# The causal mask of the second score pass: GpSimd selects on the probabilities in place of mask products on TensorE

## The chip, the cores and the metric

The kernel runs on one core of a Trainium2 chip. The metric is device time in microseconds, of one execution of the whole program. Engines are named as in the profile: PE is TensorE's products, PEld its weight loads, DVE is VectorE, ACT is ScalarE, POOL is GpSimd, SP is the queue that issues most DMAs.

## What is computed

Two blocks in a row on an input of 2 batches of 512 tokens with 128 channels. The first (an HGRN block with quantised linear layers and a conditioning path) is untouched by the change. The second is a transformer block with adaptive layer norms; its attention has 16 heads of width 8 and a causal mask:

```python
def _attention(x, Wqkv, Wproj, bproj):
    ...
    scores = jnp.einsum('bhqd,bhkd->bhqk', q, k) * scale
    causal = jnp.tril(jnp.ones((t, t), bool))
    scores = jnp.where(causal, scores, -jnp.inf)
    attn = jax.nn.softmax(scores, axis=-1)
    out = jnp.einsum('bhqk,bhkd->bhqd', attn, v)
    ...
...
x = x + gt_a[:, None, :] * _attention(xm, Wqkv, Wproj, bproj)
xn = _layernorm(x, g2, be2)
...
h = jax.nn.gelu(xm @ W1 + b1, approximate=False)
x = x + gt_m[:, None, :] * (h @ W2 + b2)
```

## The kernel before

The program is written engine by engine, with semaphores set by hand; each engine goes through its instructions in the order of the text. The attention works in 8 groups of 4 heads (2 batches, 4 groups each; `N_GROUPS`). The heads of a group stand in two halves of the partitions, rows 0 to 63 and 64 to 127, so that products of the two halves can run beside each other in PE's array. Queries and keys are split into three bf16 parts and stacked (`QS`, `KS`, 48 rows of a half).

Scores are computed twice. The **first pass** has queries on the partitions: for each group there are 12 score items (`score_item`, lines 1401 to 1403), each one score product for one or two heads and then two mask products, which add -1e30 above the diagonal. An item goes to one of three PSUM banks, and DVE takes its row maxima (`row_maxima`, line 1139). When the 12 items of a group are reduced, DVE splits the maxima into three bf16 parts by four small operations (`split_maxima`, lines 1149 to 1152), PE transposes them (`maxima`, line 1413), DVE copies them (line 1160), and SP's DMAs put them into `QS` as three more rows (line 358).

The **second pass** has keys on the partitions. Its score product (51 rows, the maxima included) gives the score less its row's maximum. It goes in 5 slots for a group (`exp_slot`): slots 0 and 1 hold key tile 0, slots 2 and 3 key tiles 1 and 3, slot 4 key tile 2. A slot fills two banks; banks 0 to 3 are used in turn by slot. Before the change each pair of tiles has a score product for either half (line 1437) and then two mask products for either half (lines 1440 and 1443), which write into the first 128 columns of the tile, the diagonal block:

```python
for half in range(2):
    rows = half_rows(2 * half, XROWS)
    T.matmul(dsts[half], KS[b][rows, h, tok(kt)], QS[b][rows, h, kt * P:L], start=True, stop=False)
for half in range(2):
    r = half_rows(2 * half)
    T.matmul(dsts[half][:, 0:P // 2], k_of("pickLo", r), k_of("maskKlo", r), start=False, stop=False)
```

ACT takes the exponential of a slot into `PT` (line 707) and counts `p_ready`. PE waits for `p_ready` of two slots before when it fills a slot again, and for the slots of a key tile before that tile's value products (`values`, line 1457; `PV_SLOTS` has the count). The value matrix carries a column of ones, so the sum of each row comes out of the same products. ACT copies the result (line 715), PE turns it (line 1290, helper `to_columns`), and DVE divides (lines 1168, 1169).

The order of the rounds is written by hand. In round n PE does the 12 score items of group n; between them stand slots 3 and 4 of group n-2 (at items 1 and 4), slots 0, 1 and 2 of group n-1 (at items 7, 9, 11), the transposes of the maxima of group n-1 (at item 2), the value products of group n-2 (key tiles 0, 1, 3, 2 at items 5, 6, 7, 10), and the turned values of group n-3 (at item 3). The loop runs on for three rounds after the last group; in round 8 PE also does the attention columns and the projection of batch 0, and at the end of round 9 the transposes of its normalised rows (`norm_columns(0)`).

POOL has little to do in this stage. It issues half of the DMAs that stack the keys, adds the projection's bias to `xs`, and later, for each batch, takes the root for the norm (line 379) when DVE has the variance (`ln_var`), waits until DVE has written the normalised rows (`xhat_ready`), and adds the bias of the MLP to `xs` (line 470).

## Time and profile before

| what | value |
|---|---|
| median of 3 runs | 289.58 us (289.57 to 290.57) |
| profiled execution, its own time | 289.72 us |
| its span in the profile | 287.60 us |
| granted TensorE clock, mean | 0.798 |
| PE / PEld busy | 160.0 us (56%) / 102.1 us (35%) |
| DVE busy | 188.6 us (66%) |
| ACT busy | 139.1 us (48%) |
| POOL busy | 69.5 us (24%) |
| chain that ended last | DVE 37%, PE 33%, DMA 10%, POOL 5%, SP 5%, ACT 4% |

Busy times are shares of the whole span. The program has stages with different limits, so these shares do not say what a change in one stage is worth. PE's products are pipelined and their ends are modelled; starts are the better guide there.

### The profile page before, as it was taken

What the parts mean: (1) busy time and instruction counts of PE and PEld (TensorE: products, weight loads), DVE (VectorE), ACT (ScalarE), POOL (GpSimd) and SP (SyncE); (2) the same over time, 40 slices, a digit from 0 to 9 for tenths busy, and PEclk for the clock granted to TensorE, in tenths of its full rate; (3) what the DMA queues carried; (4) which work ended last, traced back from release to release, by engine and by line L of the source; (5) the groups of instructions that cost most, each with busy time, mean ns of one, the idle gap of its engine ahead of it and who ended that gap; (6) DMA issues with size and microseconds to landing.
All of it is one profiled execution on the core that took longest, in us unless ns stands there. A gap on an engine that the chain in (4) does not pass through costs nothing.

```text
span 287.6 us, 4182 instructions
## 1 busy us (share of the span) xinstructions
PE 160.0 (56%) x1493; PEld 102.1 (35%) x1495; DVE 188.6 (66%) x528; ACT 139.1 (48%) x297; POOL 69.5 (24%) x77
## 2 busy tenths in 40 slices
PE   0212239444733006227580009579999999897985
PEld 0102135243512003027350006254564456354664
DVE  0687797999966985965852009657897788715320
ACT  3455877557845036933164000045466446676621
POOL 7061621326035152960168000000000000003110
PEclk9999999857555556857777555559999999999999
DMA  6992000000000000000048555500000000000010
GB/s 190 417 396 125 1 0 0 0 2 1 0 0 1 0 0 0 1 2 0 0 72 89 69 69 72 70 4 4 4 3 1 5 4 2 4 2 3 0 39 36
DMA packets 5355, 12.15 MB, mean 42 GB/s; under 512 B 1075, under 2 KB 3604, under 8 KB 4692
## 3 DMA queue, kind: packets, MB, share of 16 engines
q1 hardware_dynamic: 4758, 11.09, 14.8%
q0 software_dynamic: 576, 0.79, 2.1%
q8 instruction: 12, 0.20, 0.3%
q14 instruction: 9, 0.07, 0.1%
HBM read 8.11 MB, written 0.52 MB: 30 GB/s over the span
## 4 chain that ended last, share of the span: by engine, by line
DVE 37%; PE 33%; DMA 10%; POOL 5%; SPq 5%; ACT 4%; issue 4%; DVEq 0%; ACTq 0%
DVE negmax L1139 9%; PE ps L1457 6%; DMA KS<-part 6%; PE ps L1290 5%; SPq L326 4%; PE ps L1401 4%; POOL uh L445 3%; DMA QS<-nmT 3%; PE ps L1487 2%; PE ps L1493 2%; DMA cw<-in_cond_w 2%; PE ps L1349 2%; PE ps L1437 2%; DVE xhat L810 2%; DVE u L967 2%
## 5 line engine op out<-in xcount | busy, mean ns | idle before, releaser
L1139 DVE TENSOR_REDUCE negmax<-ps 128x1 f32<-128x384 f32 (+3 forms) x96 | 52.6, 594 | 35.7 <-PE ps L1403 35.7
L707 ACT ACTIVATE PT<-ps 128x1024 f32<-128x1024 f32 x40 | 40.7, 1026 | 63.8 <-PE ps L1443 63.6
L1401 PE MATMUL ps<-KS,QS 48*128 48x384 bf16 (+3 forms) x128 | 36.5, 344 | 21.1 <-DMA KS<-part 20.8
L379 POOL TENSOR_TENSOR rstd<-veps,mhalf 128x4 f32<-128x4 f32 x8 | 8.1, 1016 | 139.9 <-DVE veps L804 139.9
L1290 PE MATMUL ps<-k_f,u 128*128 128x128 f32 x40 | 10.0, 426 | 34.4 <-ACT u L631 23.4
L1437 PE MATMUL ps<-QS,KS 51*128 51x512 bf16 (+3 forms) x128 | 24.6, 315 | 5.1 <-DMA QS<-nmT 5.0
L1402 PE MATMUL ps<-k_b 64*128 64x128 bf16 x128 | 27.2, 245 | 0.0
L1401 PEld LDWEIGHTS ps<-KS,QS 48*128 48x128 bf16 x128 | 11.7, 100 | 37.5 <-issue 22.5
L1403 PE MATMUL ps<-k_b 64*128 64x64 bf16 x128 | 23.9, 208 | 0.0
L1457 PE MATMUL ps<-PT,V 128*9 128x512 f32 (+3 forms) x256 | 22.5, 434 | 1.9 <-ACT PT L707 1.2
L1290 PEld LDWEIGHTS ps<-k_f,u 128*128 128x128 f32 x40 | 7.6, 221 | 36.2 <-DVE u L967 28.1
L1443 PE MATMUL ps<-k_b 64*128 64x128 bf16 x128 | 18.2, 222 | 0.0
L1440 PE MATMUL ps<-k_b 64*128 64x64 bf16 x128 | 17.5, 196 | 0.0
L1403 PEld LDWEIGHTS ps<-k_b 64*128 64x128 bf16 x128 | 13.2, 111 | 6.7 <-issue 2.4
L379 POOL TENSOR_TENSOR rms<-vms,mhalf 128x4 f32<-128x4 f32 x10 | 10.2, 1033 | 21.0 <-DVE vms L941 20.8
L1220 PE MATMUL ps<-k_f,cq 2*128 2x2 f32 x14 | 2.3, 249 | 19.0 <-DVE cq L830 19.0
L810 DVE TENSOR_SCALAR xhat<-xs,bnmv,rstd 128x128 f32<-128x128 f32 x32 | 10.8, 401 | 3.0 <-POOL rstd L379 2.9
L1402 PEld LDWEIGHTS ps<-k_b 64*128 64x128 bf16 x128 | 12.2, 104 | 0.0
L1437 PEld LDWEIGHTS ps<-QS,KS 51*128 51x128 bf16 x128 | 9.4, 96 | 7.1 <-DMA QS<-nmT 6.0
L1349 PE MATMUL ps<-k_f,uh 128*128 128x128 f32 x32 | 6.4, 386 | 9.7 <-DVE uh L1102 9.7
L445 POOL TENSOR_TENSOR uh<-prod,brow 128x512 f32<-128x512 f32 x8 | 9.8, 1270 | 5.2 <-DVE prod L1089 5.2
L1443 PEld LDWEIGHTS ps<-k_b 64*128 64x128 bf16 x128 | 9.2, 98 | 3.0 <-issue 0.6
(200 smaller groups left out, 435.0 us busy)
## 6 DMA issues: line engine op xcount, KB each, us to landing
w<-in_wa SPq DMA_DIRECT2D x2, 1152.0 KB, 10.7
QS<-part SPq DMA_DIRECT2D x24, 64.0 KB
brow<-in_bcast_rows SPq DMA_DIRECT2D x1, 1152.0 KB, 15.9
lw<-in_l_w SPq DMA_DIRECT2D x1, 1152.0 KB
mw<-in_main_w SPq DMA_DIRECT2D x1, 1024.0 KB, 13.5
KS<-part POOLq DMA_DIRECT2D x12, 64.0 KB, 5.6
KS<-part SPq DMA_DIRECT2D x12, 64.0 KB
cw<-in_cond_w SPq DMA_DIRECT2D x1, 576.0 KB, 5.9
```

The lines of the kernel that those rows point to most:

```text
L379: return nc.gpsimd.tensor_tensor(r, v, mhalf[0:v.shape[0], 0:v.shape[-1]], ALU.pow)
L445: nc.gpsimd.tensor_tensor(uh[b][:, t, :], prod[b][t % 2][:, :], brow_of("nm2"), ALU.mult).then_inc(S["uh_raw"], 1)
L707: nc.scalar.activation(PT[n % 2][:, s, :], bank(2 * (use % 2), 2), ACT.Exp).then_inc(S["p_ready"], 1)
L1139: V.tensor_reduce(negmax[n % 2][:, qt, h0:h0 + nh], bank(S_BANKS[k % 3])[:, 0:nh * w].rearrange("p (h w) -> p h w", w=w), AX.X, ALU.max, n ...
L1290: ins = T.transpose(dst[:, tok(t)], src(t), ident)
L1401: T.matmul(dst, QS[b][rows, h, tok(qt)], KS[b][rows, h, 0:w], start=True, stop=False)
L1402: T.matmul(dst[:, w - P:w], k_of("pickLo", r), k_of("maskQlo", r), start=False, stop=False)
L1403: ins = T.matmul(dst[:, w - P // 2:w], k_of("pickHi", r), k_of("maskQhi", r), start=False, stop=True)
L1437: T.matmul(dsts[half], KS[b][rows, h, tok(kt)], QS[b][rows, h, kt * P:L], start=True, stop=False)
L1440: T.matmul(dsts[half][:, 0:P // 2], k_of("pickLo", r), k_of("maskKlo", r), start=False, stop=False)
L1443: ins = T.matmul(dsts[half][:, 0:P], k_of("pickHi", r), k_of("maskKhi", r), start=False, stop=True)
L1457: ins = T.matmul(bank(6)[32 * j:32 * j + HD + 1, kt * P:L], V1[b][:, kt, g * HG + j, :], src, start=(kt == 0), stop=(kt == 2))
```

## The change

The mask products of the second pass are taken out. ACT's exponential now counts `p_exp`, on which PE's reuse of the banks waits. POOL waits for the same count, sets the upper triangle of each diagonal block of `PT` to zero by `affine_select`, in place, and counts `p_ready`, on which the value products wait as before. The two mask tables of this pass leave the constants. The first pass keeps its mask products. POOL's root and addition for batch 0's norm (`norm_root(0)`) now stand behind the select of slot 2 of the last group, those of batch 1 at the end.

```diff
 KC, KC_N = _spans(("ident", P), ("pickLo", P), ("pickHi", P), ("maskQlo", P), ("maskQhi", P // 2),
-                  ("maskKlo", P // 2), ("maskKhi", P), ("count", 16))
+                  ("count", 16))
...
-            for b in range(B):
+
+            def drop_future(n, s):
+
+                diagonals = [(0, 2, L)] if s < 2 else [(0, 2, L), (3 * P, 2, L)] if s < 4 else [(0, 4, 2 * P)]
+                pool.wait_ge(S["p_exp"], 5 * n + s + 1)
+                for at, count, step in diagonals:
+                    v = PT[n % 2][:, s, :].rearrange("p (c w) -> p c w", w=step)[:, :, at:at + P]
+                    ins = nc.gpsimd.affine_select(v, v, [[0, count], [1, P]], ALU.is_ge, 0.0, base=0,
+                                                  channel_multiplier=-1)
+                ins.then_inc(S["p_ready"], 1)
+
+            def norm_root(b):
                 pool.wait_ge(S["ln_var"], 3 * B + b + 1)
                 root(rstd[:, tiles(b)], veps[:, tiles(b)]).then_inc(S["ln_root"], 1)
 
                 pool.wait_ge(S["xhat_ready"], B + b + 1)
                 nc.gpsimd.tensor_tensor(xs[:, tiles(b), :], xs[:, tiles(b), :], over_tiles(b2_g[:, b, :]), ALU.add
                                         ).then_inc(S["biased"], 1)
+
+            for n in range(N_GROUPS):
+                for s in range(5):
+                    drop_future(n, s)
+                    if n == N_GROUPS - 1 and s == 2:
+                        norm_root(0)
+            norm_root(1)
...
                 nc.scalar.activation(PT[n % 2][:, s, :], bank(2 * (use % 2), 2), ACT.Exp
-                                     ).then_inc(S["p_ready"], 1)
+                                     ).then_inc(S["p_exp"], 1)
...
                 if use >= 2:
-                    pe.wait_ge(S["p_ready"], use - 1)
+                    pe.wait_ge(S["p_exp"], use - 1)
...
-                        T.matmul(dsts[half], KS[b][rows, h, tok(kt)], QS[b][rows, h, kt * P:L], start=True, stop=False)
-                    for half in range(2):
-                        r = half_rows(2 * half)
-                        T.matmul(dsts[half][:, 0:P // 2], k_of("pickLo", r), k_of("maskKlo", r), start=False, stop=False)
-                    for half in range(2):
-                        r = half_rows(2 * half)
-                        ins = T.matmul(dsts[half][:, 0:P], k_of("pickHi", r), k_of("maskKhi", r), start=False, stop=True)
+                        ins = T.matmul(dsts[half], KS[b][rows, h, tok(kt)], QS[b][rows, h, kt * P:L],
+                                       start=True, stop=True)
                 ins.then_inc(S["st_pe"], 1)
```

How the change moves instructions is seen in the order in which they stand on an engine. First POOL, at the end of the program, before the change: L379 is the root, L470 the addition, for batch 0 and then batch 1.

```order
L463 TENSOR_TENSOR xs<-xs,bproj_g 128x512 [waits xhat_ready,gated]
L463 TENSOR_TENSOR xs<-xs,bproj_g 128x512
L379 TENSOR_TENSOR rstd<-veps,mhalf 128x4 [waits ln_var]
L470 TENSOR_TENSOR xs<-xs,b_g 128x512 [waits xhat_ready]
L379 TENSOR_TENSOR rstd<-veps,mhalf 128x4 [waits ln_var]
L470 TENSOR_TENSOR xs<-xs,b_g 128x512 [waits xhat_ready]
```

The same end after the change (L472 is the select, L481 the addition), from the first three slots of the last group on:

```order
L472 AFFINE_SELECT PT<-PT 128x2x128 [waits p_exp] x3
L472 AFFINE_SELECT PT<-PT 128x2x128
L379 TENSOR_TENSOR rstd<-veps,mhalf 128x4 [waits ln_var]
L481 TENSOR_TENSOR xs<-xs,b_g 128x512 [waits xhat_ready]
L472 AFFINE_SELECT PT<-PT 128x2x128 [waits p_exp]
L472 AFFINE_SELECT PT<-PT 128x2x128
L472 AFFINE_SELECT PT<-PT 128x4x128 [waits p_exp]
L379 TENSOR_TENSOR rstd<-veps,mhalf 128x4 [waits ln_var]
L481 TENSOR_TENSOR xs<-xs,b_g 128x512 [waits xhat_ready]
```

The selects of slots 3 and 4 of the last group stand behind an addition that waits for DVE's normalised rows. Second PE, in a round, around slot 0 of a group and the value products of key tile 3, before:

```order
L1437 MATMUL ps<-QS,KS 128x512 [waits p_ready,nm_stacked0]
L1437 MATMUL ps<-QS,KS 128x512
L1440 MATMUL ps<-k_b 128x64 x2
L1443 MATMUL ps<-k_b 128x128 x2
L1457 MATMUL ps<-PT,V 9x128 [waits p_ready]
L1457 MATMUL ps<-PT,V 9x128 x3
```

And after (L1455 is the score product, L1470 the value product):

```order
L1455 MATMUL ps<-QS,KS 128x512 [waits p_exp,nm_stacked1]
L1455 MATMUL ps<-QS,KS 128x512
L1470 MATMUL ps<-PT,V 9x128 [waits p_ready]
L1470 MATMUL ps<-PT,V 9x128 x3
L1419 MATMUL ps<-KS,QS 128x512 [waits s_used]
```

Four products between the scores and what follows are gone, and nothing else changed its place on PE.

## Rows read from the trace of the kernel before

**Rows 1.** The page: busy time, and granted clock and GB/s in 40 slices.

```profile
PE 160.0 (56%) x1493; PEld 102.1 (35%) x1495; DVE 188.6 (66%) x528; ACT 139.1 (48%) x297; POOL 69.5 (24%) x77
...
PEclk9999999857555556857777555559999999999999
...
GB/s 190 417 396 125 1 0 0 0 2 1 0 0 1 0 0 0 1 2 0 0 72 89 69 69 72 70 4 4 4 3 1 5 4 2 4 2 3 0 39 36
```

**Rows 2.** By stretch: us; PE, PEld, DVE, ACT, POOL busy; clock, DMA share, GB/s.

```profile
221.58:231.32 9.74, 9.04 (x143) 5.06 (x138) 7.86 (x20) 5.48 (x7) 0.00 (x0) 1.00 0.01 4
```

**Rows 3.** Chain of waits through one round: start, us, what.

```profile
222.78 0.39 PE ps L1413 x4
...
224.76 0.10 PE ps L1443 x2
...
226.60 0.76 PE ps L1457 x8
...
227.78 0.19 PE ps L1440
...
228.80 2.49 DVE negmax L1139 x4
```

**Rows 4.** The same chain before the projection of batch 0.

```profile
257.89 0.03 PE ps L1440 x2
257.92 0.06 PE ps L1443 x2
```

**Rows 5.** PE in order of time, slot 2 of a group: start, us, instruction.

```profile
229.87 0.33 PE L1437 MATMUL ps<-QS,KS 51*128 51x384 bf16 x1
```

**Rows 6.** POOL's instructions by form: busy us, mean ns, idle before.

```profile
L445 POOL TENSOR_TENSOR uh<-prod,brow 128x512 f32<-128x512 f32 x8 | 9.8, 1270 | 5.2 <-DVE prod L1089 5.2
L379 POOL TENSOR_TENSOR rstd<-veps,mhalf 128x4 f32<-128x4 f32 x8 | 8.1, 1016 | 139.9 <-DVE veps L804 139.9
...
L384 POOL TENSOR_SCALAR w4q<-w,whalf 128x768 bf16<-128x768 f32 x2 | 4.4, 2198 | 0.0
L374 POOL MEMSET KS<- 128x2048 f32 x2 | 3.5, 1798 | 0.0
...
L384 POOL TENSOR_SCALAR cwq<-cw,whalf 128x640 bf16<-128x640 f32 x1 | 1.9, 1890 | 2.0 <-DVE whalf L769 2.0
...
L423 POOL TENSOR_TENSOR wproj_g<-lw,gates 128x128 f32<-128x128 f32 x2 | 0.9, 462 | 0.0
```

**Rows 7.** ACT and DVE in order of time, end of one round.

```profile
230.77 1.02 ACT L707 ACTIVATE PT<-ps 128x1024 f32<-128x1024 f32 x1 [0.62 <-PE ps L1443]
...
231.32 0.17 DVE L1149 CAST nmpart<-negmax 128x16 bf16<-128x16 f32 x1
...
231.95 0.17 DVE L1152 TENSOR_TENSOR nmpart<-nmrest,nmpart 128x16 bf16<-128x16 f32 x1
```

**Rows 8.** DVE and POOL in order of time, an earlier stage.

```profile
59.77 0.17 DVE L950 SCALAR_TENSOR_TENSOR stepq<-amax,guard 128x12 f32<-128x12 f32 x1
...
65.51 1.28 POOL L427 TENSOR_TENSOR w_g<-lw,gates 128x512 f32<-128x512 f32 x1
65.61 1.21 DVE L950 SCALAR_TENSOR_TENSOR stepq<-amax,guard 128x12 f32<-128x12 f32 x1
```

**Rows 9.** POOL and PE in order of time, after the last group.

```profile
261.54 1.03 POOL L379 TENSOR_TENSOR rstd<-veps,mhalf 128x4 f32<-128x4 f32 x1 [103.97 <-DVE veps L804]
...
262.09 2.34 PE L1457 MATMUL ps<-PT,V 128*9 128x512 f32 x32 [1.20 <-ACT PT L707]
...
263.80 1.27 POOL L470 TENSOR_TENSOR xs<-xs,b_g 128x512 f32<-128x512 f32 x1 [1.23 <-DVE xhat L810]
```

**Rows 10.** PE in order of time, after an idle stretch of an earlier stage.

```profile
69.80 1.54 PE L1290 MATMUL ps<-k_f,u 128*128 128x128 f32 x6 [3.00 <-DVE u L967]
```

**Rows 11.** PE by form, 127 to 133 us, and 264 to 273 us.

```profile
L1349 PE MATMUL ps<-k_f,uh 128*128 128x128 f32 x24 | 5.4, 423 | 9.7 <-DVE uh L1102 9.7
...
L1290 PE MATMUL ps<-k_f,xhat 128*128 128x128 f32 x4 | 0.7, 286 | 0.0
```

More of the change, by code:

```diff
@@ L128 @@
     "minv_ready", "mod_copied", "mod_pe", "mod_ready", "mx_ready", "niT_pe", "ni_ready", "nm_ready", "o_ready",
-    "p_ready", "par_ready", "part0", "part1", "part2", "pr_pe", "prod_ready", "pv_pe", "pv_ready", "qk_pe",
+    "p_exp", "p_ready", "par_ready", "part0", "part1", "part2", "pr_pe", "prod_ready", "pv_pe", "pv_ready", "qk_pe",
     "rest_ready", "s_pe", "s_used", "sg_ready", "sig_ready", "silu_c", "st_pe", "stack_init", "stored", "ug_ready",
@@ L1570 @@
     mask_q = _np.where(i[None] > i[:, None], f32(BIG), f32(0))
-    mask_k = _np.where(i[:, None] > i[None], f32(BIG), f32(0))
     counts = _np.array([1.0 / WCOUNT[name] for name in WCOL] + [0.0] * (16 - len(WCOL)), f32)
@@ L1585 @@
         "rows1": _np.concatenate([a["L1_bada"][2 * D:3 * D], a["L1_bada"][5 * D:]])[None],
-        "consts": _np.concatenate([eye, eye[lo], eye[hi], mask_q[lo], mask_q[hi][:, P // 2:], mask_k[lo][:, :P // 2],
-                                   mask_k[hi], _np.broadcast_to(counts, (P, 16))], 1),
+        "consts": _np.concatenate([eye, eye[lo], eye[hi], mask_q[lo], mask_q[hi][:, P // 2:],
+                                   _np.broadcast_to(counts, (P, 16))], 1),
     }
```

## The prediction

> **What bounds the kernel now.** I read the page first. No engine is full over the span [rows 1], so an average tells little and the stage has to be looked at. The change works in the attention stage, from about 189 us on. Its rounds are alike: one of the five full ones stands in the table by stretch [rows 2]; each is 9.74 us with DVE busy 7.86 us and PE busy about 9 (pipelined, so not at its peak), and POOL not at all. The chain of waits through one round then says who ends last [rows 3]: it goes through DVE from the first 512-wide reduction of a round (228.80) over the four small splitting operations to the first reduction behind them, and through PE from the transposes of the maxima (222.78) to 228.80. So what PE does between 222.78 and 228.80 is on the path, and what it does beside the four long reductions and the splitting operations is not.
>
> **Mask products off PE.** A group has 8 pairs of score blocks (one block in each half), each with 2 mask products a half: 32 products leave each group, 256 in all, with their weight loads. The two halves stand in different rows of the array and run beside each other, so a pair costs what one half costs. Two clean pieces of the chain show it: 0.03 + 0.06 = 0.09 us from the end of the score product to the next work [rows 4]. In the PE stretch of a round lie slot 4 (two pairs, chain piece 224.76) and slot 0 (one pair, 227.78); slots 1, 2 and 3 lie beside DVE's reductions, slot 2 at 229.87 for instance [rows 3, 5]. That is 3 x 0.09 = 0.27, I take 0.28 us for each of six rounds (groups 2 to 7): **-1.7 us**. The first round runs at half the clock and is partly DVE-bound; I give it **-0.2**. The last round waits for a DMA of the maxima, which hides what was saved before it; the four pairs between it and the projection (0.37 us) I count in the tail below.
>
> **Smaller constants.** 192 columns of 784 go, 98 KB. The second weight load lands behind them and ACT waits for it; the page's slices moved 190 to 417 GB/s [rows 1], so 98 KB are 0.24 to 0.5 us: **-0.2**. The cast of the constants is shorter too, on an idle DVE, worth nothing. No DMA is passed: POOL's stacking DMAs stand ahead of the selects.
>
> **What a select costs.** The trace has none. The nearest rows are POOL's [rows 6]: two-input operations of 512 elements 1.27 us and of 128 elements 0.47, so 2.1 ns an element and 0.73 us for 256; a one-input comparison of 768 in 2.20, of 640 in 1.89, so 2.4 ns an element, 0.97 us for 256 and 1.58 for 512; a fill of 2048 in 1.80, which leads to about 0.3 and 0.5. I take 0.85 us for 256 and 1.43 for 512, between the two that read; the fill, which reads nothing, and the comparison are the ends. What speaks for something far dearer is the power function, 1.02 us for four elements. The Trainium skill (GPSIMD Engine Reference, Engine selection) calls one-input work "roughly line-rate"; at the 1.2 GHz it gives, that would be an estimated 0.2 us and the issue for 256, near the fill and against the comparison's row. By that page the sum below would end near 291.
>
> **Does POOL keep up?** Seven selects in a group, six of 256 and one of 512: 6 x 0.85 + 1.43 = 6.5 us of a 9.7 us round. The tight place is slot 3. Slot 2's exponential ends at 231.79 in the round shown [rows 7]; the value products that want slot 3 start at 226.60 in this round [rows 3], so at 236.34 in the next; between them POOL has four selects, 4.5 us, so a select may cost 1.1 us before PE waits. PE's own bank reuse waits for the exponential alone and is untouched. So in a round these waits are hidden; cover gone, they cost 4c - 4.5 us a round.
>
> **The new collision.** Slot 2's exponential ends at 231.79, and without the masks of slots 1 and 2 (3 x 0.09 us of PE work before it) near 231.5. POOL then starts two selects. DVE's four splitting operations run from 231.32 to 232.12 [rows 7], and two of them read two tiles of SBUF. The trace of another stage shows what happens then [rows 8]: the small operation of line 950 takes 0.17 us when POOL is idle and 1.21 us when it starts 0.10 us behind a POOL operation of 1.28 us: it is held until that one ends. Line 1152 would start at 231.95 and be held to 231.55 + 0.85 = 232.40: 0.45 us, on the chain, in six rounds: **+2.7**. Nothing if the select falls behind it; if line 1150 is caught as well, up to one more select, 1.3 us a round. The Trainium skill (SBUF — State Buffer, Who interferes with whom) goes further: copies and casts that enter a two-port mode are held as well. The casts of lines 1149 and 1151 have no row beside a busy POOL; by that page the collision would be nearer the dear end, some 2 to 5 us more in the sum.
>
> **The tail.** This is the largest term. The changed order on POOL puts the root and the addition of batch 0's norm ahead of the selects of the last group's slots 3 and 4. The root waits for DVE's statistics and starts at 261.54, the addition waits for the normalised rows, starts at 263.80 and takes 1.27 us, ending at 265.07 [rows 9]. With the 0.37 us from the mask products before the projection (257.89 and its like, [rows 4]) it ends at 264.70. Only then come two selects of slot 3, to 266.40. The value products of key tile 1 (0.76 us) start, key tile 3 follows (0.34); slot 4's select ends at 267.83; key tile 2 (0.55, from the like rows of a round) is done at about 268.45. Before, the 32 value products ended at 262.09 + 2.34 = 264.43 [rows 9]. Everything behind them (PE's in-order queue: the transposes of batch 0's normalised rows, those of the values, the projection of batch 1, the MLP) waits for PE: **+4.0 us**, from 2.6 with selects priced as the fill to 4.4 with those priced as the comparison.
>
> **The clock.** In that tail PE stands idle for some 3.8 us, and before that for 1.2 as now [rows 9]. Earlier in the run an idle of 3.00 us that ended at 69.80 [rows 10] took the granted clock down: PEclk in the page is 7 in the slice around it and 5, the lower of the two levels (1.2 instead of 2.4 GHz), in the five slices behind it [rows 1]. A 128x128 f32 product takes 423 ns at the low level and 286 at the high one [rows 11], some 1.5 times. With four to five us of such work at the low level, of which part is hidden: **+1.5**, from 0 to 3.
>
> **Sum.** -1.7 - 0.2 - 0.2 + 2.7 + 4.0 + 1.5 = +6.1 us. The profiled execution took 289.72 us (span 287.60 and 2.12 around it), 0.14 above the median of 289.58, which I leave out. 289.7 + 6.1 = **295.8 us**.
>
> **Rivals.** *The collision misses.* The selects start behind line 1152 or do not hold it; the end of slot 2's exponential is only 0.16 us from that line's start now. Then -2.1 + 4.0 + 1.0 gives 292.6; with selects priced as the fill, 2.6 of tail and 0.5 of clock, 290.7. *POOL becomes the bound.* With a select of 1.5 us (2.6 for the wide one) POOL needs 11.6 us a round, two more than now: 6 x 2 for rounds, 5 to 6 in the tail and 3 for clock and collision give about 310. It decides from 1.1 us a select; POOL's idle column and the comparison row speak against it, the power function for it. *Faster.* The mask products give back more than the chain says: PE's work beside the reductions counts too, so that all 8 pairs of a group shorten a round, 8 x 0.09 = 0.72 us, in seven rounds 5.0. With selects priced as the fill, tail 2.6 and clock 0.5, no collision, the time is 289.7 - 0.4 - 5.0 + 3.1 = 287.4. It decides where the gain of a round passes 0.4 us. Against it: beside the reductions PE waits for DVE's banks, not DVE for PE, since DVE's idle time of a round lies before 228.80 and not behind it.
>
> **Chances and range.** A measurement of this kernel tells about 0.5% (1.45 us) from no change. Forecast 0.58, collision missed 0.21 (0.06 of it within 0.5%), POOL the bound 0.13, faster 0.08 (0.06 beyond 0.5%, 0.02 within). That is faster 0.06, same 0.08, slower 0.86. The forecast's own ends: low with a light collision 292; high with 4.4 of tail, 3 of clock and a collision of 1.1 us in six rounds, 6.6: -2.1 + 14.0, 301.6. The range reaches to 290.8 for the missed collision and to 303 for a POOL that just binds; what lies outside is the faster case and most of the POOL-bound one, about 0.2.
>
> **What would show it.** Right: rounds of about 9.9 us instead of 9.74, with DVE's line 1152 at 0.5 to 0.7 us instead of 0.17 and the transposes of the maxima later by that; selects at 0.7 to 1.0 us; in the tail, selects directly behind the b2 addition, PE idle for over 3 us between the first and the second set of value products and waiting for POOL, and a granted clock below 1.00 behind it. Wrong: a round shorter than 9.5 us with line 1152 at 0.17 (collision missed); rounds over 10.5 us with POOL near full and PE waiting for selects inside them; or no PE wait for POOL in the tail, which would take the largest term away.

## The result and the profile after

| | before | after |
|---|---|---|
| median of 4 runs each | 289.57 us (289.02 to 290.57) | 299.27 us (298.16 to 303.03) |
| ratio | | 1.032 (1.027 to 1.037) |
| profiled execution, its span | 289.72 us, 287.6 us | 298.16 us, 296.0 us |
| granted TensorE clock, mean | 0.798 | 0.758 |

The changed kernel is slower by 3.2%. Measured once more in a later session it took 300.54 us against 288.82 (ratio 1.035, 1.027 to 1.043). The forecast was 295.8 us in a range of 290.8 to 303.0: the sign and roughly the size came out, but two large terms were missing that nearly cancel. Ratios leave out runs over 1.5% above the fastest of their kernel, which flatters a kernel whose own runs spread further than that, so medians of all runs stand beside them.

The spans show the two missing terms. They are cut at three events that both traces have: the first score product of the second pass, DVE's first splitting operation of group 1, and DVE's first splitting operation of the last group. The last stretch, from that operation to the end, is called the tail below, and times "in the tail" count from it.

| stretch | before | after | difference | forecast |
|---|---|---|---|---|
| start of the program to the first score product of the second pass | 188.90 | 179.81 | -9.1 | -0.2 |
| to the first splitting operation of group 1 | 3.91 | 3.75 | -0.2 | -0.2 |
| six rounds, to the first splitting operation of group 7 | 57.99 | 70.02 | +12.0 | +1.0 |
| tail | 36.8 | 42.4 | +5.6 | +5.5 |
| sum | 287.6 | 296.0 | +8.4 | +6.1 |

The page of the changed kernel, the lines that answer to [rows 1]; the fourth line is the group of all selects:

```profile
PE 171.3 (58%) x1237; PEld 97.4 (33%) x1239; DVE 191.2 (65%) x528; ACT 138.3 (47%) x297; POOL 93.3 (32%) x133
...
PEclk9999999756655558667975555598777796895999
...
GB/s 184 409 403 88 1 0 0 0 3 0 0 1 0 0 0 1 0 2 0 50 101 87 88 98 7 4 1 3 2 3 2 4 0 4 2 3 0 0 38 35
...
L472 POOL TENSOR_SCALAR_AFFINE_SELECT PT<-PT 128x256 f32<-128x256 f32 (+1 forms) x56 | 23.8, 439 | 83.8 <-ACT PT L725 83.8
```

PE has 256 products fewer and is busy 11.3 us longer. That contradiction is the first thing to see: the products that stay must have become slower. The clock's digits say why. In [rows 1] they are 9 from 195 us on to the end; now the slices of the rounds have 6 to 9, most of them 7 or 8.

**The rounds.** By stretch, two rounds of the changed kernel (the columns of [rows 2]: us; PE, PEld, DVE, ACT, POOL busy; granted clock, DMA share, GB/s):

```profile
206.42:217.49 11.07, 10.07 (x106) 4.71 (x104) 8.36 (x19) 5.38 (x7) 2.98 (x7) 0.85 0.01 3
217.49:230.01 12.52, 11.52 (x106) 5.08 (x104) 8.46 (x19) 5.39 (x7) 2.98 (x7) 0.73 0.01 2
```

Against [rows 2], a round has its 32 mask products fewer (a window's count takes in a few at its edges) and lasts 1.3 to 2.8 us longer, and its mean clock is 0.85 or 0.73 where it was 1.00. POOL is busy 2.98 us of 11 to 12.5, so it bounds nothing. Cut finer, the same view shows a mean of 0.85 to be one stretch of 3.4 us at the lower level, 1.2 GHz (in the rounds at 0.73 it is 6.8 us):

```profile
207.00:208.00 1.00, 0.14 (x4) 0.14 (x4) 0.96 (x4) 1.00 (x2) 0.45 (x2) 1.00 0.00 0
208.00:209.00 1.00, 1.00 (x12) 0.76 (x11) 1.00 (x4) 0.02 (x1) 0.77 (x2) 0.88 0.00 0
209.00:210.00 1.00, 1.00 (x6) 0.51 (x5) 0.84 (x3) 0.00 (x0) 0.00 (x0) 0.50 0.00 0
210.00:211.00 1.00, 1.00 (x14) 0.61 (x15) 0.96 (x4) 0.15 (x1) 0.00 (x0) 0.50 0.02 6
211.00:212.00 1.00, 1.00 (x8) 0.00 (x0) 0.49 (x1) 0.87 (x1) 0.06 (x1) 0.50 0.02 6
212.00:213.00 1.00, 1.00 (x11) 0.33 (x11) 0.10 (x1) 0.00 (x0) 0.57 (x1) 0.91 0.00 0
213.00:214.00 1.00, 1.00 (x13) 0.26 (x5) 0.46 (x1) 0.00 (x0) 0.00 (x0) 1.00 0.00 0
```

The fall comes behind PE's one wait of the round. In order of time on PE that wait is this row, 0.86 us before the transposes of the maxima:

```profile
207.87 0.39 PE L1431 MATMUL ps<-k_b,nmpart 128*12 128x128 bf16 x4 [0.86 <-DVE negmax L1157]
```

Before, the same wait was 0.61 us (213.04 us and the same place of the other rounds), and the clock stayed at 1.00. From round to round the fall comes 0.1 to 1.8 us behind the end of this wait. So the trace alone leaves two suspects: a longer wait, or fewer products around it.

**The collision.** DVE in order of time at the end of one round, then POOL at the same time:

```profile
217.49 0.17 DVE L1167 CAST nmpart<-negmax 128x16 bf16<-128x16 f32 x1
217.70 0.18 DVE L1168 TENSOR_TENSOR nmrest<-negmax,nmpart 128x16 f32<-128x16 f32 x1
217.91 0.28 DVE L1169 CAST nmpart<-nmrest 128x16 bf16<-128x16 f32 x1
218.23 0.32 DVE L1170 TENSOR_TENSOR nmpart<-nmrest,nmpart 128x16 bf16<-128x16 f32 x1
...
217.76 0.76 POOL L472 TENSOR_SCALAR_AFFINE_SELECT PT<-PT 128x256 f32<-128x256 f32 x2 [1.06 <-ACT PT L725]
```

It happens, at the instruction that was named: L1170 (the old L1152) takes 0.32 us where [rows 7] have 0.17. The cast of L1169 is held too, 0.28 instead of 0.17. Together that is 0.11 + 0.15 = 0.26 us more a round, where 0.45 was forecast.

**The tail.** PE in order of time behind the last group (the rows that answer to [rows 9]), then POOL:

```profile
266.25 1.43 PE L1470 MATMUL ps<-PT,V 128*9 128x512 f32 x8 [1.12 <-DVE attn L1187]
270.01 2.75 PE L1470 MATMUL ps<-PT,V 128*9 128x384 f32 x24 [2.33 <-POOL PT L472]
...
265.71 1.04 POOL L379 TENSOR_TENSOR rstd<-veps,mhalf 128x4 f32<-128x4 f32 x1 [1.26 <-DVE veps L822]
267.98 1.26 POOL L481 TENSOR_TENSOR xs<-xs,b_g 128x512 f32<-128x512 f32 x1 [1.23 <-DVE xhat L828]
269.19 1.36 POOL L472 TENSOR_SCALAR_AFFINE_SELECT PT<-PT 128x256 f32<-128x256 f32 x3
```

The selects stand directly behind the b2 addition (the addition of the MLP's bias), and PE waits 2.33 us for them, with 24 of the 32 value products behind the wait. Stretches of 2 us show PE idle throughout 268 to 270. The clock is at its lower level there, but it fell before this wait began, at 266.78 us, which is why the first stretch has 0.70:

```profile
266.00:268.00 2.00, 1.43 (x8) 0.15 (x8) 1.22 (x5) 0.20 (x1) 0.77 (x2) 0.70 0.00 0
268.00:270.00 2.00, 0.00 (x0) 0.00 (x0) 0.00 (x0) 0.00 (x0) 2.00 (x4) 0.50 0.00 0
270.00:272.00 2.00, 1.99 (x20) 0.76 (x24) 0.00 (x0) 0.00 (x0) 0.55 (x1) 0.50 0.00 0
```

**The start.** The chain of waits runs through the stacking DMAs in both kernels; first the last piece of one wait in the changed kernel:

```profile
154.64 12.72 DMA KS<-part
```

and the same piece before:

```profile
156.13 15.96 DMA KS<-part
```

A second piece of this kind, DMA QS<-nmT, takes 6.27 us before and 1.91 after and ends at 188.86 and at 179.76. So of the 9.1 us 1.5 lie ahead of the first piece, 3.2 in it and 4.4 in the second. The GB/s of the full slices there are 69 to 89 before [rows 1] and 87 to 101 after. The stacking, which the change doesn't touch, landed sooner.

### The profile page after: what moved, and what is told of

Its sections match the earlier page's. It is cut to its first block, busy times and chain, and to the rows that moved or that the text cites. A ratio compares the mean times of both kernels' runs of the same rounds, so it can differ in the third digit from the quotient of the medians.

```text
span 296.0 us, 3727 instructions
## 1 busy us (share of the span) xinstructions
PE 171.3 (58%) x1237; PEld 97.4 (33%) x1239; DVE 191.2 (65%) x528; ACT 138.3 (47%) x297; POOL 93.3 (32%) x133
## 4 chain that ended last, share of the span: by engine, by line
DVE 40%; PE 35%; DMA 8%; POOL 7%; issue 4%; ACT 4%; SPq 2%; DVEq 0%
DVE negmax L1157 9%; PE ps L1470 9%; PE ps L1308 5%; DMA KS<-part 4%; PE ps L1419 4%; POOL uh L445 3%; DMA w<-in_wa 3%; PE ps L1500 2%; PE ps L1506 2%; DVE xhat L828 2%; PE ps L1455 2%; DVE bnst L815 2%; DVE u L985 2%; DVE mx L1068 2%; PE ps L1367 1%
## 5 line engine op out<-in xcount | busy, mean ns | idle before, releaser
L472 POOL TENSOR_SCALAR_AFFINE_SELECT PT<-PT 128x256 f32<-128x256 f32 (+1 forms) x56 | 23.8, 439 | 83.8 <-ACT PT L725 83.8
L1419 PE MATMUL ps<-KS,QS 48*128 48x128 bf16 (+3 forms) x128 | 40.4, 371 | 16.4 <-DMA KS<-part 15.4
L1470 PE MATMUL ps<-PT,V 128*9 128x512 f32 (+3 forms) x256 | 32.6, 600 | 4.0 <-POOL PT L472 2.3
L1420 PE MATMUL ps<-k_b 64*128 64x128 bf16 x128 | 29.6, 261 | 0.0
L1421 PE MATMUL ps<-k_b 64*128 64x64 bf16 x128 | 25.6, 220 | 0.0
L1455 PE MATMUL ps<-QS,KS 51*128 51x512 bf16 (+3 forms) x128 | 25.0, 340 | 0.6 <-DMA QS<-nmT 0.6
L379 POOL TENSOR_TENSOR rstd<-veps,mhalf 128x4 f32<-128x4 f32 x8 | 8.3, 1036 | 40.6 <-DVE veps L822 40.6
L1421 PEld LDWEIGHTS ps<-k_b 64*128 64x128 bf16 x128 | 14.5, 120 | 9.3 <-issue 5.3
L379 POOL TENSOR_TENSOR rms<-vms,mhalf 128x4 f32<-128x4 f32 x10 | 10.2, 1031 | 21.0 <-DVE vms L959 20.8
L1420 PEld LDWEIGHTS ps<-k_b 64*128 64x128 bf16 x128 | 12.7, 107 | 1.4 <-issue 0.6
L1367 PE MATMUL ps<-k_f,uh 128*128 128x128 f32 x32 | 5.6, 350 | 9.7 <-DVE uh L1120 9.7
L604 ACT ACTIVATE junk<-mx 128x128 f32<-128x128 f32 x16 | 4.7, 297 | 11.1 <-DVE mx L954 11.1
L379 POOL TENSOR_TENSOR cs<-cs,mhalf 2x1 f32<-2x1 f32 x6 | 3.4, 558 | 20.7 <-DVE cs L838 20.7
L1455 PEld LDWEIGHTS ps<-QS,KS 51*128 51x128 bf16 x128 | 8.5, 101 | 3.2 <-issue 2.2
## 6 DMA issues: line engine op xcount, KB each, us to landing
w<-in_wa SPq DMA_DIRECT2D x2, 1152.0 KB, 10.5
```

The lines of the kernel that those rows point to most:

```text
L379: return nc.gpsimd.tensor_tensor(r, v, mhalf[0:v.shape[0], 0:v.shape[-1]], ALU.pow)
L472: ins = nc.gpsimd.affine_select(v, v, [[0, count], [1, P]], ALU.is_ge, 0.0, base=0, channel_multiplier=-1)
L1419: T.matmul(dst, QS[b][rows, h, tok(qt)], KS[b][rows, h, 0:w], start=True, stop=False)
L1420: T.matmul(dst[:, w - P:w], k_of("pickLo", r), k_of("maskQlo", r), start=False, stop=False)
L1421: ins = T.matmul(dst[:, w - P // 2:w], k_of("pickHi", r), k_of("maskQhi", r), start=False, stop=True)
L1455: ins = T.matmul(dsts[half], KS[b][rows, h, tok(kt)], QS[b][rows, h, kt * P:L], start=True, stop=True)
```

## The experiments

Each ratio is against the kernel before in the same session (medians 288.40 to 288.82 us), with its 95% interval. The medians are of all runs; for the close cases both are read.

**e1: selects kept, mask products put back.** The changed kernel's order, waits and POOL work, with the four mask products of a pair and their two tables as before.

```diff
-                        ins = T.matmul(dsts[half], KS[b][rows, h, tok(kt)], QS[b][rows, h, kt * P:L],
-                                       start=True, stop=True)
+                        T.matmul(dsts[half], KS[b][rows, h, tok(kt)], QS[b][rows, h, kt * P:L], start=True, stop=False)
+                    for half in range(2):
+                        r = half_rows(2 * half)
+                        T.matmul(dsts[half][:, 0:P // 2], k_of("pickLo", r), k_of("maskKlo", r), start=False, stop=False)
+                    for half in range(2):
+                        r = half_rows(2 * half)
+                        ins = T.matmul(dsts[half][:, 0:P], k_of("pickHi", r), k_of("maskKhi", r), start=False, stop=True)
```

> The changed kernel with the mask products of the second pass and their tables put back: PE works as before the change, POOL selects as after it. Theory (the clock): the slower rounds of the changed kernel come from the granted clock, which falls when PE has less to do; with the products back it stays at 1.00 in the rounds, a round takes 9.74 us plus what the selects cost DVE's splitting operations (0 to 0.3 us), and the sum is 289.6 + 6 x 0.2 + the tail behind the root and addition (about 3) = 294. Rival (the selects): the selects themselves stretch the rounds, by holding DVE or PE; then a round stays at 11 to 12.5 us and the time stays at 299 or goes above it.

Measured: 292.77 us (290.91 to 293.66), ratio 1.013 (1.007 to 1.019). Two of its rounds, by stretch, and PE's wait in the first of them:

```profile
207.79:217.70 9.91, 9.05 (x143) 5.06 (x138) 8.03 (x19) 5.48 (x7) 2.97 (x7) 1.00 0.01 3
217.70:227.60 9.90, 9.04 (x143) 5.05 (x138) 8.03 (x19) 5.47 (x7) 2.98 (x7) 1.00 0.02 4
...
209.15 0.39 PE L1431 MATMUL ps<-k_b,nmpart 128*12 128x128 bf16 x4 [0.77 <-DVE negmax L1157]
```

256 more products, and the kernel is 6.5 us faster than the changed one's 299.27. Its start was 3.2 us later than the changed kernel's (182.98 against 179.81 us), so the gain doesn't come from there: its six rounds take 60.5 us against 70.0. All its rounds from the second of the six on are 9.90 us at clock 1.00. PE waits 0.77 us in them, longer than the 0.61 of before, and the clock holds. POOL works as long as in the changed kernel, so POOL is not what lengthens the rounds there. What is left over 9.74 is 0.17 us, the collision: in its rounds only the last splitting operation is held (0.34 us instead of 0.17), since with the masks back the selects start later against the splitting. The tail stays long (43.3 us), as it should with the order on POOL unchanged; PE waits 2.71 us for the selects in it, and the clock is at its lower level for 10.2 us from the midst of that wait.

**e2: no masks and no selects.** The kernel before with the mask products taken out and nothing in their place; the exponential's scale is set to 0.1 so that future tokens do not overflow. The second pass is then not causal.

```diff
-                        T.matmul(dsts[half], KS[b][rows, h, tok(kt)], QS[b][rows, h, kt * P:L], start=True, stop=False)
...
+                        ins = T.matmul(dsts[half], KS[b][rows, h, tok(kt)], QS[b][rows, h, kt * P:L], start=True, stop=True)
```

> The kernel before without the mask products of the second pass and without selects, so that the second pass has no causal mask; the exponential's scale is 0.1 so that its values stay finite. POOL does nothing in the rounds. Theory (the clock): the granted clock falls in the rounds as in the changed kernel, rounds of 10.5 to 12 us, about 297 in all. Rival (the selects): rounds shorten to about 9.45 us as the chain of the kernel before says, and the time is 289.6 - 2 = 287.5.

Measured: 294.30 us (289.72 to 297.41, 10 runs), ratio 1.013 (1.008 to 1.018). Work was taken away, none was added, and it is slower than before. Two of its rounds, by stretch:

```profile
223.97:233.63 9.66, 8.62 (x106) 4.27 (x104) 7.87 (x20) 5.39 (x7) 0.00 (x0) 1.00 0.01 2
233.63:244.40 10.77, 10.02 (x106) 4.73 (x104) 8.10 (x20) 5.39 (x7) 0.00 (x0) 0.84 0.01 3
```

The clock falls without any POOL work, and with PE's wait for the maxima at 0.61 us as before. So the fewer products are enough, and the wait of 0.86 us isn't needed for it; nor is a longer wait alone enough, by the 0.77 us of e1. Over its ten executions the mean granted clock was 0.762 to 0.794, over the 13 of the kernel before 0.793 to 0.815, so this is no matter of the one trace. Its rounds swing between 9.66 at 1.00 and 10.77 at 0.84; those of the changed kernel go down to 0.73, which the longer wait behind the collision may explain; fewer products with nothing but a longer wait weren't run. The row at full clock carries a second result: taking the masks away is worth 9.74 - 9.66 = 0.08 us a round, not 0.28. PE in order of time says where the rest went, first the value products of key tile 0 in the round of [rows 2], then the same in this one:

```profile
225.21 1.04 PE L1457 MATMUL ps<-PT,V 128*9 128x512 f32 x8
...
227.59 1.05 PE L1451 MATMUL ps<-PT,V 128*9 128x512 f32 x8 [0.30 <-DVE attn L1169]
```

PE now comes to the value products before DVE has divided the previous group's turned values, which lie in the same bank, and waits 0.30 us for it. No full round of the kernel before has this wait. Against the first splitting operation of the round the value products start at 3.63 us before (225.21 - 221.58) and at 3.62 here (227.59 - 223.97): taking away the two pairs of masks of slot 4, which stand ahead of them, gained nothing. The one pair of slot 0 stands behind them and gave the 0.08: the next 512-wide reduction of DVE starts at 7.22 us before (228.80) and 7.14 here (231.11).

**e4: filler products.** The changed kernel with six 512-column products a round, whose results nobody reads, ahead of the transposes of the maxima, so that PE's wait there is filled (0.21 us of it are left).

```diff
+            def filler(n):
+                use = 5 * n + 4
+                pe.wait_ge(S["p_exp"], use - 1)
+                for half in (0, 1) * 3:
+                    r = half_rows(2 * half, SROWS)
+                    T.matmul(bank(2 * (use % 2) + half), KS[0][r, 0, tok(0)], QS[0][r, 0, :], start=True, stop=True)
...
+                    if i == 2 and 2 <= n < N_GROUPS:
+                        filler(n - 2)
```

> The changed kernel with six 512-column products a round that nobody reads (rounds 2 to 7), written into the banks of slot 4 ahead of its scores, where PE waits for DVE anyway (before the transposes of the maxima): per half 1536 columns, as many as the mask products had. Theory (the clock): the granted clock stays at 1.00 in the rounds, rounds of 9.7 to 9.9 us instead of 11.0 to 12.5, 299.3 - 6 x 1.7 = 289 and with the tail unchanged at 292 at most. Rival: the work to no purpose lengthens PE's queue by 0.2 to 0.6 us a round and the clock stays as it is: 300 to 303.

Measured: 293.29 us (290.82 to 296.00), ratio 1.013 (1.007 to 1.020). A round, by stretch:

```profile
205.95:215.86 9.91, 9.25 (x112) 4.53 (x110) 8.13 (x19) 5.39 (x7) 2.98 (x7) 1.00 0.01 3
```

Six useless products bring the clock back to 1.00 and take up to 2.6 us off a round; the median stays above the 289 to 292 us that were expected, because the tail stays long. e1 and e4 restore the clock by different products at different places. e4 shortens PE's wait as well, e1 hardly does; what they share is that PE has more to do. The Trainium skill (TensorE: Matmul & The Clock Gate, A second HAM failure mode) tells of a kernel whose short idles between groups of products let the clock swing between its two levels; the rounds of e2 agree. The same page's advice against idle gaps of several us (Why this matters for your kernels) would not have warned here: PE's longest wait in a round was 0.86 us.

**e3: the root last.** In the changed kernel, the root and addition of batch 0 moved behind all selects.

```diff
-                    if n == N_GROUPS - 1 and s == 2:
-                        norm_root(0)
-            norm_root(1)
+            for b in range(B):
+                norm_root(b)
```

> The changed kernel with the root and the addition of batch 0's norm behind the selects of the last group's slots 3 and 4. Theory: the value products of the last group no longer wait for the addition; PE's idle of 2.33 us in front of them falls below 0.5, the addition moves off the chain, and the root starts 0.5 to 1.5 us later. The tail gives back 3 to 5 us: 295 to 296. Rival: the root on POOL is what the norm waits for, so what the values gain the norm loses, and the time is within 1 us of the changed kernel's 299.

Measured: 297.67 us (296.41 to 299.86), ratio 1.032 (1.026 to 1.038); the tail is 40.05 us against 42.4. PE in order of time:

```profile
267.26 4.03 PE L1469 MATMUL ps<-PT,V 128*9 128x512 f32 x32 [1.36 <-DVE attn L1186]
```

The wait for POOL is gone and all 32 value products run together, but almost all of them at the lower clock (from 267.52 to 270.94 us): 4.03 us for what took 2.34 [rows 9]. The clock took 1.7 us of the gain, and less was gained than expected. So the clock falls in this tail with the long wait for POOL gone; the wait isn't needed for it.

**f4: both, filler and root last.** The edits of e3 and e4 together.

> The changed kernel with both repairs: the six products a round to no purpose ahead of the transposes of the maxima, and the root and addition behind the last selects. Theory: the two gains add up; rounds of 9.91 us at a clock of 1.00, and from the last round's end to the end of the program 40 us instead of 43.2, so about 290. Rival: with PE no longer waiting for POOL something else holds the tail (the DVE's division and the clock), and less than 1.5 us come back: 292.

Measured: 289.90 us (285.30 to 292.12, 10 runs) against 288.74, ratio 0.996 (0.988 to 1.003). The same row, now:

```profile
262.64 2.34 PE L1476 MATMUL ps<-PT,V 128*9 128x512 f32 x32 [1.37 <-DVE attn L1186]
```

2.34 us again, and the tail is 37.9 us against 43.2 in e4. With clock and order mended, the kernel is level with the one before. Of the 5.3 us between e4 and f4, 1.4 are not the order's: the projection of batch 0 began 9.59 us into the tail in e4 and 8.17 in f4, because the clock was low for longer there (6.8 us in e4, 3.4 in f4). Some 3.9 us are left for the order.

**g1: no collision.** f4, and POOL waits for the last splitting operation before the selects of slot 2.

```diff
+                if s == 2 and n + 1 < N_GROUPS:
+                    pool.wait_ge(S["nm_ready"], n + 2)
```

> The same as the kernel with both repairs, and POOL holds slot 2's selects of a group back until DVE's four splitting operations of the next group are done. Theory (collision): the operations of lines 1169 and 1170 go back from 0.28 and 0.32 us to 0.17, and a round from 9.91 to 9.66 us, the round of the kernel without masks and selects at full clock; 1.5 us less in all, 288.5. Rival: the 0.25 us a round come from somewhere else (the filler, the slots' new timing); the operations get short, the rounds stay at 9.9.

Measured: 288.24 us (285.25 to 291.20, 10 runs) against 288.74, ratio 0.993 (0.989 to 0.997). DVE and POOL in order of time, end of a round:

```profile
228.71 0.17 DVE L1170 CAST nmpart<-nmrest 128x16 bf16<-128x16 f32 x1
228.91 0.18 DVE L1171 TENSOR_TENSOR nmpart<-nmrest,nmpart 128x16 bf16<-128x16 f32 x1
...
229.22 1.51 POOL L474 TENSOR_SCALAR_AFFINE_SELECT PT<-PT 128x256 f32<-128x256 f32 x4 [1.72 <-DVE nmpart L1171]
```

Both held operations are back at 0.17 and 0.18 us, and the five rounds at full clock are 9.65 to 9.66 us instead of 9.91: the collision costs 0.25 us a round, cast included. The rounds show this; the medians of f4 and g1 alone would not, since their intervals overlap. The Trainium skill (SBUF — State Buffer, Who interferes with whom) names copies and casts among the work that a busy GpSimd can hold; the two traces agree, 0.28 us beside a select and 0.17 without.

**h1: fillers in the tail too.** g1, with six fillers more before slot 0 of the last group's second pass and six before its value products.

> The kernel with both repairs and without the collision (rounds of 9.65 us), with two more sets of six products to no purpose, ahead of slot 0 of the last group (where PE waits for the DMA of the maxima) and ahead of its value products (where it waits for DVE). Theory (clock): the granted clock stays at 1.00 behind 250 us as in the kernel before, and the stretch from the last round to the end falls by 1 us or more. Rival: the clock there was hardly low, the two sets only lengthen the queue, and the time is the same within 0.5 us or 0.5 to 1 us longer.

Measured: 289.15 us (285.09 to 291.52, 10 runs) against 288.43, ratio 0.994 (0.989 to 0.999); the tail is 38.36 us, 0.64 longer than in g1. The expected gain did not come, the rival did. The clock is at its lower level for the same 3.4 us as in g1, 1.3 to 4.7 us into the tail, ahead of both sets, which therefore could not help it. The first set delays what follows by 0.65 us, since PE has no wait there in g1; the second stands inside a wait of 1.37 us and delays nothing more.

**f3 and f2: why did the second pass start early?** f3 is the changed kernel with 192 columns that nobody reads put back into the constants, so that load, cast and the places of all later tiles are as before. f2 keeps the small load and pads only the two tiles, so the places alone are as before. The edit shown is that of f2.

```diff
-        k_f = sb("k_f", [P, KC_N])
-        k_b = sb("k_b", [P, KC_N], BF16)
+        k_f = sb("k_f", [P, KC_N + 192])[:, 0:KC_N]
+        k_b = sb("k_b", [P, KC_N + 192], BF16)[:, 0:KC_N]
```

> The changed kernel with 192 columns that nobody reads in the constants, so that their load, their cast and the place of every later tile in SBUF are as before the change. Theory (the smaller constants did it): the second pass of group 0 starts near 183 to 189 instead of 180, and the time rises from 299 to about 304. Rival (run to run, or the load alone at 0.2 us): it starts near 180, and the time stays within 1 us of 299.

> The changed kernel with 192 columns of SBUF left empty behind each of the two constants' tiles, so that every later tile lies where it lay before the change; load and cast stay small. Theory (the place): the second pass of group 0 starts near 188 as with the dead columns, and the time is near 303. Rival (the load, 98 KB early in the run): it starts near 180 to 184 as in the changed kernel, and the time is near 299.

Measured: f3 303.03 us (301.39 to 304.59), ratio 1.049 (1.042 to 1.056), second pass from 187.67 us. f2 301.20 us (299.90 to 301.84), ratio 1.041 (1.035 to 1.047), second pass from 186.49 us. Each was in its own session as slow as or slower than the changed kernel in its sessions, and the interval of f3 lies above the changed kernel's first one (up to 1.037) and barely meets that of the repeat (1.027 to 1.043). That speaks for a part of the early start that is not chance. Some of their rounds ran at 1.00 and took 9.91 to 9.92 us, the length of a round of the changed kernel at full clock.

**i1 and f1: the two kernels once more.**

> The changed kernel once more, for a second trace. Theory: rounds of 11.0 to 12.5 us at a granted clock of 0.85 and 0.73 as in its first trace, with perhaps one at 9.9 where the clock stays up, 42 us from the last round's first splitting operation to the end. The start of the second pass of group 0, 179.81 us in its first trace, is the open point: near 180 again if it belongs to the kernel, anywhere from 180 to 188 if it differs from run to run. About 299 in all.

> The kernel before once more, for a second trace of it. In its first trace the second pass of group 0 started at 188.90 us, in that of the changed kernel at 179.8. Theory (the smaller constants did it, through the place of the tiles or the load): it starts near 188 again. Rival (the landing of the stacking DMAs differs from run to run): it starts anywhere between 179 and 189.

Measured: i1 is the repeat told of in the result; its second pass began at 183.72 us, not 179.81, and its rounds were again 11.02 to 12.55 us at 0.85 or 0.73 but for the first. f1, one run, took 290.70 us, second pass from 188.35 us, rounds of 9.73 behind a first one of 10.91 at clock 0.74. So 4 us of the 9.1 were particular to one execution or one session.

**h2: the kernel before, its mask tables loaded late.** The two tables get their own DMA behind the stacking and tiles behind all others; masks stay on PE.

```diff
-                    sp.dma_start(k_f[:, :], consts).then_inc(S["ld_const"], 16)
+                    sp.dma_start(k_f[:, :], consts[:, 0:KC_N]).then_inc(S["ld_const"], 16)
...
+            sp.dma_start(mk_f[:, :], consts[:, KC_N:KC_N + MK_N]).then_inc(S["ld_mk"], 16)
```

> The kernel before with the two mask tables of the second pass taken out of the constants, loaded by a DMA of their own behind the stacking DMAs, into tiles behind all others, and cast on POOL. All mask products stay, no selects. Theory (load or place of the constants): the second pass of group 0 starts 4 to 8 us earlier than the 188 to 189 of the kernel before, and the time falls to 283 to 286. Rival (chance between runs): it starts within 1 us of 188, less 0.2, plus what the new DMA adds, and the time is within 1 us of the kernel before.

Measured: 286.80 us (285.34 to 288.80, 10 runs) against 288.43, ratio 0.994 (0.990 to 0.998). The second pass began at 186.14 us, 2 to 3 us earlier than in the two traces of before; rounds and tail are those of before. It is faster by some 0.6%: less than the 4 to 8 us that the theory asked for, more than the rival allowed. f2 and h1, whose first load is as small, started at 186.49 and 186.19 in the same session, but no kernel with the whole load was traced in it, so how much of the 2 to 3 us belongs to the session can't be said.

The starts of the second pass, one trace each, in us:

| constants and places | runs |
|---|---|
| small, shifted | after 179.81, e4 180.09, e3 180.73, i1 183.72, g1 184.25, f4 184.51, h1 186.19 |
| small, places as before | f2 186.49 |
| as before | before 188.90, f1 188.35, e2 187.85, f3 187.67, e1 182.98 |
| late tables (h2) | 186.14 |

The means of the first and third lines are 182.8 and 187.2. Within a line the starts differ by 6 us, and e1 lies with the first line though its constants are large. Part of that goes with the session: e1 to e4 were measured in one (small 180.09 and 180.73, as before 182.98 and 187.85), f1, f3, f4 and g1 in a second (small 184.25 and 184.51, as before 187.67 and 188.35), and f2, h1 and h2 in a third (186.14 to 186.49). In the first two the small constants start 2.3 us or more ahead. In the third all three kernels load few constants at first and start alike, although the places of their tiles differ. The traces show that the difference lies in when the DMAs that stack the keys and the maxima land; they don't say whether the size of the load, the place of the tiles, the session or chance decides it. **This stays open.**

## Why the prediction came out as it did

- **Direction and time.** Slower was right, and 299.3 lies inside the range, 3.5 us above the forecast. It was right partly by luck: 11 us missing in the rounds and 9 us missing at the start.
- **Mask products off PE, -1.7 us: the step that failed.** Two things were wrong. First its size: at full clock a round gained 0.08 us (e2), not 0.28. Of the three pairs counted on the path the two of slot 4 gave nothing, because the value products behind them start no earlier: they wait for DVE's division. I asked what the masks cost on the path and not what would be late next. Second, and larger, its price: I put the risk of the clock only where PE would stand idle for several us, in the tail, and took a round's clock of 1.00 as given. With the masks gone it falls in every round but few. A round of this kernel at full clock is 9.91 us, so six should take 59.5; they took 70.0. That is **10.6 us for the clock** in the profiled execution. Of these 8.8 lie in the last five rounds, which e1, e4, f4 and g1 hold at 1.00. The other 1.8 are in the first, and cannot all be put on the masks: in it the clock still comes up from the low level in every run (mean 0.88 before and 0.74 in f1, 0.65 after, 0.73 in e1). The other 1.5 over the 58.0 of before are the collision (six times 0.25), less the gain of 0.08 each, and a first round that before was only 9.30.
- **Smaller constants, -0.2 us.** The second pass began 9.1 us earlier in the profiled execution and 4.6 in the repeat (183.72 against 188.35 in f1). Part of that is chance or session; the rest is open, as said.
- **A select.** It was priced at 0.85 and 1.43 us. It took:

```profile
L472 POOL TENSOR_SCALAR_AFFINE_SELECT PT<-PT 128x256 f32<-128x256 f32 x48 | 18.8, 407 | 65.2 <-ACT PT L725 65.2
...
L472 POOL TENSOR_SCALAR_AFFINE_SELECT PT<-PT 128x512 f32<-128x512 f32 x8 | 5.1, 635 | 18.6 <-ACT PT L725 18.6
```

  That is 0.89 ns an element and 0.18 us around it. It is the fill's rate in [rows 6] (1.80 us for 2048, 0.88 ns), not the comparison's 2.4. I had leaned to the operations that read; the low end was right, and the Trainium skill's "roughly line-rate" (GPSIMD Engine Reference, Engine selection), which the prediction quoted, was nearer than the row that I took. The rival of POOL as the bound falls with it: 2.98 us of a round.
- **The collision, +2.7 us.** The right instruction, the right neighbour, and 0.25 us a round instead of 0.45 (the full-clock rounds of f4 against g1), some 1.5 us in six. The 0.45 was a slip: it is the whole length of the held operation, 231.95 to 232.40, of which it takes 0.17 anyway (to 232.12). By the prediction's own prices the delay was 0.28 us a round, +1.7 in all. That this is near the 0.25 is luck as well: the holding select is half as long as priced, and the cast is held too, which the prediction had kept for the dear end.
- **The tail, +4.0 us.** Root and addition ahead of the selects did what was said. An estimate from the rows: had the clock stayed up, the addition would end as before at 14.27 us in the tail, two selects at 15.04, the 24 products (2.11 us in e4) at 17.15, against 13.63 before: 3.5 us, and some 3.9 by e4 and f4. Cheap selects make it less than 4.0.
- **The clock in the tail, +1.5 us.** It was 2.0: 0.64 in the 24 products (2.75 against 2.11) and 1.4 ahead of the projection, where the clock was 0.64 and 0.51 in 256 to 260 us. The second place wasn't foreseen; it is that of the rounds again. And the cause given, PE's idle of 3.8 us (2.33 was measured), was not what took the clock down: it fell at 266.78 us, before the wait for POOL, and it falls in e3 without that wait. The size came out near by luck.
- **The other rivals.** "Collision misses" and "faster" are both out: no round was shorter than 11.03 us in the profiled execution. No rival named what happened. The signs that I set down did catch it: "rounds over 10.5 us" came, but with POOL a quarter busy, so the sign pointed to a cause that wasn't there.

Undone piece by piece, the medians go back to the level of before: clock (after to e4, 299.3 or 300.5 to 293.3), order on POOL (to f4, 289.9), collision (to g1, 288.2). g1 with everything mended is at best 0.7% faster than before by its ratio, and 0.2% by the medians. Its six rounds take 59.6 us and its tail 37.7, neither less than before; what it has ahead of it is its start at 184.25 us (188.35 in f1, the kernel before in the same session). The masks were nearly free where they stood, and on PE they also kept the clock up. Of all versions h2, which leaves them there, has the lowest median (286.8 us).

## What to carry to other kernels

Where PE is busy nine tenths of a loop at full clock, look at its granted clock as a resource of its own: products taken off it can cost more than they save. Price the removal at both levels, and try it alone, without the new work, before building its replacement. Work put on a strictly ordered queue must not stand behind something that waits for a later stage: one root and one addition ahead of three cheap selects cost some 3.5 to 4 us. And a saving on a chain is worth only the distance to the next wait; name that wait before counting the saving.

## What the runs showed of the hardware

- The granted clock fell to its lower level (0.50) for 3.4 us at a time, or 6.8, although PE never idled longer in a full round than 0.61 us (e2) or 0.86 us (after), and came back by itself. With 32 short mask products more a round the clock held 1.00, at a wait of 0.61 us (before) and of 0.77 (e1).
- Six 512-column products a round, with no reader, brought it back to 1.00 and were worth 1.1 to 2.6 us a round (e4).
- A group of 32 value products took 4.03 us in e3, 3.4 of them at the lower clock, and 2.34 at the upper (before, f4): 1.7 times.
- A GpSimd select in place on f32 takes 0.41 us for 128x256 and 0.64 us for 128x512; a comparison to bf16 on the same engine took 2.20 us for 128x768 [rows 6].
- Casts of 16 elements on DVE are held by a GpSimd select, 0.17 to 0.28 us, and two-input operations 0.18 to 0.32.
- The same stacking DMAs ended up to 9 us apart between kernels that differ in 192 columns of constants, and 4 us apart between two executions of one kernel in different sessions (after and i1).
